# Graph attention on one core: three chunks instead of one gathered in the stage ahead of each layer

## The chip, the cores and the metric

The kernel runs on one core of one Trainium2 chip, in one launch. The metric is the device time of an execution in microseconds. PE is the matrix engine (PEld its weight loads), DVE the vector engine, ACT the scalar engine, POOL GpSimd, SP the sync engine. A q behind a name (POOLq, SPq, ACTq) is that engine's instruction queue. Stages are named by the kernel's functions.

## What is computed

x is 6250 x 256. It is normalised, goes through two graph attention convolutions (4 heads of 64, 100,000 edges sorted by destination, a self loop for every node) and, beside them, a linear attention; the sum is added to x, and a mixture of 16 experts with a last normalisation follows. The change lies in the edges of the two convolutions:

```python
h = (x @ W).reshape(-1, H, C)
e = leaky_relu(alpha_s[src] + alpha_d[dst], NEG_SLOPE)
ex = exp(e - segment_max(e, dst)[dst])
alpha = ex / (segment_sum(ex, dst)[dst] + 1e-16)
out = segment_sum(h[src] * alpha[:, :, None], dst).reshape(-1, H * C) + b
```

## The kernel before

The program is a row of stages, each a block in which the five engines run programs of their own and wait for each other by semaphores. At the end of a stage all engines meet at a barrier; only then does the next begin. The order is prepare, project_inputs, then for each of the two layers **bounds**, **maxima** and **gat_edges**, and last order, experts and finish. maxima does nothing here but read a flag.

Edges are worked off in NC = 98 chunks of CE = 1024 (8 columns of 128). For a chunk SP loads 1024 source indices (idx, line 905) and the destination codes (line 909). POOL then issues 8 indirect DMAs (gather_rows, line 949); each fetches 128 rows of 260 floats, h and alpha_s, from the table of the layer into gathered. There are SLOTS = 3 slots of idx and gathered: chunk c uses slot c % 3, so chunk c can be gathered once chunk c - 3 has been scaled, which the semaphore scaled counts (it starts at 3). DVE makes the selection matrices (lines 1001 and 1019), adds the logits (lines 1013 to 1015, t_e), ACT takes their exponentials (lines 1144 and 1145), DVE scales the gathered rows by them (line 1026), PE sums them per destination (line 1275), and DVE adds the sums to acc (line 1034). Between chunks, per tile of 128 nodes, stand the steps that finish a tile (ACT stores it in the table of the next layer, or in xf_d and moe_d), the linear attention in layer 0 and the gate in layer 1. PE runs spare products (line 1249) while it waits.

The steps of an engine are laid out by skewed: stages with offsets, the first and last turns written out, the middle as a loop over 6 chunks. The number of passes over all chunks is read at run time; with these inputs it is one. At the end of a pass POOL and SP do what the next pass needs (next_dests, next_load), also when there is no next one.

The first chunk of a layer is treated apart. In bounds, where DVE computes bounds of the logits, SP loads idx for chunk 0 (line 577) and POOL gathers it (line 583). In gat_edges gather and load therefore skip chunk 0, and the end of a pass loads and gathers slot 0 again: next_dests waits for the scaling of all chunks, then issues 8 gathers, then waits for the last store (semaphore stored) and computes the next destinations (lines 964 and 945). The last thing POOL does in the stage is to wait until these gathers have landed.

At the start of gat_edges DVE multiplies acc by the nodes' own weights (line 990, four instructions) before its first chunk. In layer 1 ACT issues three loads of expert weights w1, four experts each (line 1197), before its first exponentials:

```python
act.wait_ge(s["codes_in1"], 16)
act.wait_ge(s["idx_in2"], 16)
for e in range(0, NX - 4, 4):
    act.dma_start(w1[:, e:e + 4, :, :], a["L0_ffn_w1"][e:e + 4].rearrange("e (k p) f -> p e k f", p=P)).then_inc(weights_in, 16)
```

Of the kernel before, what the change touches and what calls it, by code (L numbers as in the profile page):

```python
# [33 lines left out]
KT = 8  # L34
CE = KT * P
SLOTS = 3
NC = -(-E // CE)
# [19 lines left out]
def hold(eng, sem, value, tick):  # L57

    eng.wait_ge(sem, value)
    eng.sem_inc(tick, 1)  # L60
# [75 lines left out]
def build(nc, a, out):  # L136
# [6 lines left out]
    srcp = scratch("srcp", (NC * CE,), I32)  # L143
# [6 lines left out]
    weights_in = nc.alloc_semaphore(name="weights_in")  # L150
    firsts = [(nc.alloc_semaphore(name=f"ahead{l}_idx_in0"), nc.alloc_semaphore(name=f"ahead{l}_g_half0"), nc.alloc_semaphore(name=f"ahead{l}_g_in0")) for l in range(2)]

    with ExitStack() as top:
# [20 lines left out]
        landed = sb("landed", [1, 2, XT], I32)  # L174
# [58 lines left out]
        stage(finish, a, moe_d, out, eps, ident, acc)  # L233
    nc.clear_and_free_semaphores([weights_in, *firsts[0], *firsts[1]])

# [317 lines left out]
def bounds(nc, layer, ident, ones, acc, dtab, own, peak, parts, wide, srcp, table, idx, G, ahead, sem):  # L553
# [5 lines left out]
    with ExitStack() as ctx:  # L559
# [15 lines left out]
        @block.sync  # L575
        def _(sp):
            sp.dma_start(idx[:, 0, :], srcp[0:CE].rearrange("(p t) -> p t", t=KT)).then_inc(ahead[0], 16)

        @block.gpsimd
        def _(pool):  # L580
            pool.wait_ge(ahead[0], 16)
            for k in range(KT):
                pool.indirect_dma_start(out=G[:, 0, k, :], out_offset=None, in_=table,
                                        in_offset=bass.IndirectOffsetOnAxis(ap=idx[:, 0, k:k + 1], axis=0)).then_inc(ahead[1 + 2 * k // KT], 16)

# [185 lines left out]
def gat_edges(nc, layer, srcp, table, idx, G, ahead, codes_d, partition, iota, acc, own, peak, parts, windows, attention, last, sem):  # L771
# [6 lines left out]
    with ExitStack() as ctx:  # L778
# [34 lines left out]
        else:  # L813
# [8 lines left out]
            def part(n):  # L822
# [17 lines left out]
            one = sb("one", [P, NT])  # L840
        names = ["idx_in1", "idx_in2", "g_half1", "g_half2", "g_in1", "g_in2", "codes_in0", "codes_in1", "hotT", "hotf", "targets", "dwin", "own", "own_weights",
                 "own_terms", "target_read", "logits", "weights", "scaled", "added", "acc", "pass", "dests", "dest_steps", "vsteps", "logit_steps", "tick",
# [7 lines left out]
        s = {n: sem(f"g{layer}_{n}") for n in names}  # L850
        s["idx_in0"], s["g_half0"], s["g_in0"] = ahead
        FIRST = len(range(0, NC, SLOTS))
        block = ctx.enter_context(nc.Block())
        assert NC == 2 * NT
        PER_STORE = 16 if attention else 32

        def chunks(eng, begin, end, *stages):


            rounds = eng.value_load(passes[0:1, 0:1], min_val=1, max_val=NT + 1)  # L860
            with eng.Fori(0, rounds) as r:
                def told(step):
                    return lambda c, k, u: step(r * NC + c, c, k % SLOTS, k % 2, r * len(range(k % SLOTS, NC, SLOTS)) + u * 2 + k // SLOTS)

                def tile_of(step):

                    def even(c, k, u):
                        if k % 2 == 0:
                            b = k // 2
                            step(r * NT + (u * SLOTS + b), u * SLOTS + b, b, r * len(range(b, NT, SLOTS)) + u)  # L870
                    return even
                begin(r)
                skewed(eng, NC, 2 * SLOTS, 2, 2, [(o, tile_of(step) if by_tile else told(step)) for o, step, *by_tile in stages])
                end(r)
            return rounds
# [20 lines left out]
        def _(sp):  # L896
            def next_load(r):
                hold(sp, s["logits"], r * NC + NC + SLOTS, s["tick"])
                sp.dma_start(idx[:, 0, :], srcp[0:CE].rearrange("(p t) -> p t", t=KT)).then_inc(s["idx_in0"], 16)

            def load(g, c, q, par, use):
                if isinstance(c, int) and c == 0:
                    return
                hold(sp, s["logits"], g + 1, s["tick"])
                sp.dma_start(idx[:, q, :], srcp[ds(c * CE, CE)].rearrange("(p t) -> p t", t=KT)).then_inc(s[f"idx_in{q}"], 16)
# [35 lines left out]
        def _(pool):  # L941
# [10 lines left out]
            def gather(g, c, q, par, use):  # L952
                if isinstance(c, int) and c == 0:
                    return
                pool.wait_ge(s[f"idx_in{q}"], 16 * use + 16)
                hold(pool, s["scaled"], g + 1, s["tick"])
                gather_rows(q)

            def next_dests(r):
                hold(pool, s["idx_in0"], r * (16 * FIRST) + 16 * FIRST + 16, s["tick"])  # L960
                hold(pool, s["scaled"], r * NC + NC + SLOTS, s["tick"])
                gather_rows(0)
                hold(pool, s["stored"], r * (PER_STORE * NT) + PER_STORE * (NT + 1), s["tick"])
                pool.tensor_scalar(behind[:], behind[:], -SPREAD, None, ALU.add).then_inc(s["dest_steps"], 1)
                hold(pool, s["dest_steps"], r + 2, s["tick"])
                dests()
# [3 lines left out]
            dests()  # L970
            rounds = chunks(pool, nothing, next_dests, (0, gather))
            for landed in (s["g_half0"], s["g_in0"]):
                hold(pool, landed, rounds * (8 * KT * FIRST) + 8 * KT, s["tick"])

# [850 lines left out]
```

## Time and profile before

| | |
|---|---|
| median of 3 executions | 2938.16 us (2934.69 to 2940.9) |
| the profiled execution | 2947.23 us, its span 2945.6 us |
| busy, share of the span | PE 78%, PEld 62%, DVE 62%, ACT 31%, POOL 67% |
| mean clock granted to PE | 0.951 |
| gathers | 16 in bounds (line 583), 1568 in gat_edges (line 949) |
| stages, from the timeline | layer 0: bounds from 164.6, gat_edges from 181.9; layer 1: bounds from 1264.0, gat_edges from 1280.8 |

The page gives busy shares over the whole span; they are means over stages with different limits. The busiest engine by these is PE, but a good part of its work are spare products. What bounds a stage is read from who waits for whom in it, and at its borders from the timeline.

### The profile page before, as it was taken

To read this page: it belongs to the slowest core of one execution; us is meant where nothing else is said; L and a number is where in the kernel's file an instruction comes from. 1 tells how busy PE (TensorE), PEld (TensorE's weight loads), DVE (VectorE), ACT (ScalarE), POOL (GpSimd) and SP (SyncE) were. 2 spreads that over 40 slices of the span, in tenths; PEclk is the share of its full clock that TensorE was granted. 3 is DMA by queue.
4 is the path that set the end of the run, shared out by engine and by line. 5 is a ranking of instruction groups with operands and counts; after the bars stand their busy time and mean duration, and the time that the engine had idled before them with its cause. 6 is when DMAs were issued, how large, how long until landed. Compare 5 with 4: busy or idle time off the path is not lost. (4 is left out here: it accounts for less than half of the span.)

```text
span 2945.6 us, 56016 instructions
## 1 busy us (share of the span) xinstructions
PE 2306.1 (78%) x12223; PEld 1818.2 (62%) x12224; DVE 1827.1 (62%) x4382; ACT 925.0 (31%) x2254; POOL 1959.0 (67%) x1934
## 2 busy tenths in 40 slices
PE   1737887878788787728888888888888749999996
PEld 0525555555555555526666666766676539999984
DVE  5655666666666666556666666666666574555545
ACT  0512333333333333301222222222222224444445
POOL 0357777777777777557777777777777406666654
PEclk9969999999999999969999999999999879999998
DMA  3734555555555555345555555555555355565555
GB/s 69 228 102 134 140 139 138 137 138 142 141 139 141 137 137 141 88 152 154 156 150 155 149 153 149 160 148 154 150 155 150 95 149 98 103 107 102 102 90 182
DMA packets 274989, 401.59 MB, mean 136 GB/s; under 512 B 91136, under 2 KB 187799, under 8 KB 274905
## 3 DMA queue, kind: packets, MB, share of 16 engines
q0 software_dynamic: 102496, 253.89, 34.7%
q1 hardware_dynamic: 128745, 101.18, 13.2%
q10 hardware_dynamic: 43680, 45.76, 4.8%
q8 instruction: 25, 0.41, 0.1%
q14 instruction: 43, 0.35, 0.0%
HBM read 346.42 MB, written 54.62 MB: 136 GB/s over the span
## 5 line engine op out<-in xcount | busy, mean ns | idle before, releaser
L949 POOL DMA_INDIRECT gathered<-table,idx x1568 | 1591.8, 1015 | 506.6 <-issue 438.2
L1275 PE MATMUL psA_e<-scaled,hotf 128*128 128x260 f32 x3136 | 748.1, 392 | 67.6 <-issue 62.9
L1275 PEld LDWEIGHTS psA_e<-scaled,hotf 128*128 128x128 f32 x3136 | 588.9, 193 | 159.2 <-issue 74.1
L1249 PE MATMUL psA_e<-mixM,ident 128*128 128x256 f32 x1372 | 348.0, 391 | 91.4 <-DVE hotf L1019 85.2
L1249 PEld LDWEIGHTS psA_e<-mixM,ident 128*128 128x128 f32 x1372 | 254.0, 193 | 153.9 <-issue 122.9
L1144 ACT ACTIVATE scaled<-t_e 128x32 f32<-128x32 f32 x196 | 45.0, 230 | 807.6 <-DVE t_e L1015 801.6
L1688 POOL DMA_INDIRECT moe_d<-xscaled,xtarget x113 | 179.4, 1587 | 122.9 <-DVE xtarget L1632 52.0
L1019 DVE TENSOR_TENSOR hotf<-iota,code_r 128x1024 f32<-128x1024 bf16 x196 | 240.7, 1228 | 0.0
L1026 DVE TENSOR_TENSOR scaled<-gathered,psDW_e 128x2048 f32<-128x2048 f32 x98 | 223.8, 2283 | 25.5 <-ACT psDW_e L1145 25.5
L1026 DVE TENSOR_TENSOR scaled<-gathered,psW_e 128x2048 f32<-128x2048 f32 x98 | 223.7, 2283 | 22.0 <-ACT psW_e L1145 21.5
L1013 DVE TENSOR_TENSOR z_e<-both_e,gathered 128x32 f32<-128x32 f32 x196 | 38.2, 195 | 312.7 <-DMA gathered<-table,idx 302.6
L1660 PEld LDWEIGHTS xpsH<-xxT,w1e 128*128 128x128 f32 x1808 | 220.6, 193 | 6.2 <-ACT xxT L1589 0.4
L1669 PE MATMUL xpsO<-w,hidT 128*128 x904 | 216.0, 382 | 7.4 <-DVE hidT L1621 7.2
L1660 PE MATMUL xpsH<-xxT,w1e 128*128 128x128 f32 x1808 | 221.3, 276 | 0.0
L1034 DVE SCALAR_TENSOR_TENSOR acc<-psA_e,lower,acc 128x260 f32 x196 | 95.8, 489 | 149.7 <-issue 149.4
L1621 DVE TENSOR_SCALAR hidT<-xpsH,b1T 128x128 f32<-128x128 f32 x452 | 127.5, 344 | 91.5 <-issue 46.0
L1144 ACT ACT_TABLE_LOAD x95 | 121.9, 1283 | 195.5 <-DVE t_e L1015 166.5
L1669 PEld LDWEIGHTS xpsO<-w,hidT 128*128 128x128 f32 x904 | 162.8, 190 | 29.2 <-issue 11.1
L1249 PE MATMUL psA_e<-wext,ident 128*128 128x256 f32 x588 | 165.0, 391 | 3.4 <-DVE hotf L1019 3.4
L1283 PE MATMUL psKV<-w 128*128 128x512 f32 x196 | 104.3, 658 | 70.3 <-DVE t_e L1015 70.1
L1289 PE MATMUL psKV<-w 128*128 128x512 f32 x196 | 103.4, 652 | 66.2 <-DVE t_e L1015 66.2
L1249 PEld LDWEIGHTS psA_e<-wext,ident 128*128 128x128 f32 x588 | 112.8, 199 | 64.3 <-issue 55.0
(319 smaller groups left out, 3186.4 us busy)
## 6 DMA issues: line engine op xcount, KB each, us to landing
w<-codes_d SPq DMA_DIRECT2D x196, 256.0 KB, 3.7
gathered<-table,idx POOLq DMA_INDIRECT x1584, 3.3
w<-in_L_ffn_w ACTq DMA_DIRECT2D x8, 2048.0 KB, 19.6
xb<-in_L_ffn_b SPq DMA_DIRECT2D x113, 128.0 KB
table<-acc POOLq DMA_DIRECT2D x49, 130.0 KB
table<-acc ACTq DMA_DIRECT2D x49, 130.0 KB, 2.3
xnT_d<-xnT ACTq DMA_DIRECT2D x49, 128.0 KB, 1.8
w<-xnT_d SPq DMA_DIRECT2D x49, 128.0 KB, 3.7
```

What stands on the lines that cost most here:

```text
L949: pool.indirect_dma_start(out=G[:, q, k, :], out_offset=None, in_=table, in_offset=bass.IndirectOffsetOnAxis(ap=idx[:, q, k:k + 1], axis=0 ...
L1019: dve.tensor_tensor(hotf[:, q, :, :], iota[:].rearrange("p (k f) -> p k f", k=1).to_broadcast([P, KT, P]), code_r[:, ds(c * KT, KT)].rearr ...
L1026: dve.tensor_tensor(scaled[:, par, :, 0:C].rearrange("p k (h c) -> p k h c", h=H), f, w, ALU.mult).then_inc(s["scaled"], 1)
L1144: act.activation(scaled[:, par, :, C:GW], t[:], ACT.Exp).then_inc(s["weights"], 1)
L1249: pe.matmul(psA[:, q, 0:C], ident[:], idle_rhs, start=True, stop=True)
L1275: ins = pe.matmul(psA[:, q, 0:GW], hotf[:, q, k, :], scaled[:, par, k, :], start=(k == 0), stop=(k == KT - 1))
L1283: ins = pe.matmul(psKV[:, 1, :], xnT[b][:, kc * P:(kc + 1) * P], wkvT[:, kc, 1, :], start=(kc == 0), stop=(kc == 1))
L1289: ins = pe.matmul(psKV[:, 0, :], xnT[b][:, kc * P:(kc + 1) * P], wkvT[:, kc, 0, :], start=(kc == 0), stop=(kc == 1))
L1621: dve.tensor_scalar(hidT[:, q % 2, k * P:(k + 1) * P], psH[:, q % 2, k * P:(k + 1) * P], b1T[:, ds(e, 1), k:k + 1].rearrange("p o k -> p ( ...
L1660: ins = pe.matmul(psH[:, q % 2, k * P:(k + 1) * P], w1e[:, q % 2, kc, k * P:(k + 1) * P], xT[:, q % 2, kc, :], start=(kc == 0), stop=(kc = ...
L1669: ins = pe.matmul(psO[:, q % 2, 0:C], hidT[:, q % 2, k * P:(k + 1) * P], w2[:, ds(e, 1), k, :].rearrange("p o f -> p (o f)"), start=(k == ...
L1688: pool.indirect_dma_start(out=moe_d, out_offset=bass.IndirectOffsetOnAxis(ap=target[:, q % 2:q % 2 + 1], axis=0), in_=scaled[:, q % 2, :], ...
```

## The change

The three slots are treated alike. bounds loads and gathers chunks 0, 1 and 2. In gat_edges load and gather skip chunks 0 to 2. The end of a pass loads and gathers three chunks in place of one, in the order of the slots 2, 0, 1 (numbers 98, 99, 100 modulo 3), each as soon as its own slot is free. The semaphores for idx and for the landed gathers of all three slots now live across the stages, one set for each layer. POOL's last wait covers all three slots.

```diff
-    firsts = [(nc.alloc_semaphore(name=f"ahead{l}_idx_in0"), nc.alloc_semaphore(name=f"ahead{l}_g_half0"), nc.alloc_semaphore(name=f"ahead{l}_g_in0")) for l in range(2)]
+    firsts = [{f"{n}{q}": nc.alloc_semaphore(name=f"ahead{l}_{n}{q}") for q in range(SLOTS) for n in ("idx_in", "g_half", "g_in")} for l in range(2)]
 
     with ExitStack() as top:
         def sb(name, shape, dt=F32, ctx=top):
...
         @block.sync
         def _(sp):
-            sp.dma_start(idx[:, 0, :], srcp[0:CE].rearrange("(p t) -> p t", t=KT)).then_inc(ahead[0], 16)
+            for q in range(SLOTS):
+                sp.dma_start(idx[:, q, :], srcp[q * CE:(q + 1) * CE].rearrange("(p t) -> p t", t=KT)).then_inc(ahead[f"idx_in{q}"], 16)
 
         @block.gpsimd
         def _(pool):
-            pool.wait_ge(ahead[0], 16)
-            for k in range(KT):
-                pool.indirect_dma_start(out=G[:, 0, k, :], out_offset=None, in_=table,
-                                        in_offset=bass.IndirectOffsetOnAxis(ap=idx[:, 0, k:k + 1], axis=0)).then_inc(ahead[1 + 2 * k // KT], 16)
+            for q in range(SLOTS):
+                pool.wait_ge(ahead[f"idx_in{q}"], 16)
+                for k in range(KT):
+                    pool.indirect_dma_start(out=G[:, q, k, :], out_offset=None, in_=table,
+                                            in_offset=bass.IndirectOffsetOnAxis(ap=idx[:, q, k:k + 1], axis=0)).then_inc(ahead[f"g_half{q}" if 2 * k < KT else f"g_in{q}"], 16)
...
-        s["idx_in0"], s["g_half0"], s["g_in0"] = ahead
-        FIRST = len(range(0, NC, SLOTS))
+        s.update(ahead)
...
+        def uses_of(q):
+
+            return len(range(q, NC, SLOTS))
+
+        def chunks(eng, begin, end, *stages, head=2):
 
 
             rounds = eng.value_load(passes[0:1, 0:1], min_val=1, max_val=NT + 1)
...
             def next_load(r):
-                hold(sp, s["logits"], r * NC + NC + SLOTS, s["tick"])
-                sp.dma_start(idx[:, 0, :], srcp[0:CE].rearrange("(p t) -> p t", t=KT)).then_inc(s["idx_in0"], 16)
+                for c in range(NC, NC + SLOTS):
+                    q = c % SLOTS
+                    hold(sp, s["logits"], r * NC + c + 1, s["tick"])
+                    sp.dma_start(idx[:, q, :], srcp[q * CE:(q + 1) * CE].rearrange("(p t) -> p t", t=KT)).then_inc(s[f"idx_in{q}"], 16)
 
             def load(g, c, q, par, use):
-                if isinstance(c, int) and c == 0:
+                if isinstance(c, int) and c < SLOTS:
                     return
...
             def gather(g, c, q, par, use):
-                if isinstance(c, int) and c == 0:
+                if isinstance(c, int) and c < SLOTS:
                     return
                 pool.wait_ge(s[f"idx_in{q}"], 16 * use + 16)
                 hold(pool, s["scaled"], g + 1, s["tick"])
                 gather_rows(q)
 
             def next_dests(r):
-                hold(pool, s["idx_in0"], r * (16 * FIRST) + 16 * FIRST + 16, s["tick"])
-                hold(pool, s["scaled"], r * NC + NC + SLOTS, s["tick"])
-                gather_rows(0)
+                for c in range(NC, NC + SLOTS):
+                    q = c % SLOTS
+                    hold(pool, s[f"idx_in{q}"], r * (16 * uses_of(q)) + 16 * uses_of(q) + 16, s["tick"])
+                    hold(pool, s["scaled"], r * NC + c + 1, s["tick"])
+                    gather_rows(q)
...
-            rounds = chunks(pool, nothing, next_dests, (0, gather))
-            for landed in (s["g_half0"], s["g_in0"]):
-                hold(pool, landed, rounds * (8 * KT * FIRST) + 8 * KT, s["tick"])
+            rounds = chunks(pool, nothing, next_dests, (0, gather), head=SLOTS)
+            for q in range(SLOTS):
+                for landed in (s[f"g_half{q}"], s[f"g_in{q}"]):
+                    hold(pool, landed, rounds * (8 * KT * uses_of(q)) + 8 * KT, s["tick"])
```

POOL's instructions at the stage of the bounds of layer 0 (line 583, now 585, is the gather; line 559 the end of the block, 165 the barrier, 680 or 682 the start of maxima). Before:

```order
L467 DMA table<-acc 128x260
L435 UNCONDITIONAL_BRANCH
L165 ISA
L579 UNCONDITIONAL_BRANCH
L583 DMA gathered<-table,idx 128x260 x8
L559 UNCONDITIONAL_BRANCH
L165 ISA
L680 UNCONDITIONAL_BRANCH
```

The change:

```order
L467 DMA table<-acc 128x260
L435 UNCONDITIONAL_BRANCH
L165 ISA
L580 UNCONDITIONAL_BRANCH
L585 DMA gathered<-table,idx 128x260 x24
L559 UNCONDITIONAL_BRANCH
L165 ISA
L682 UNCONDITIONAL_BRANCH
```

The gathers ahead of the barrier are 24 in place of 8.

POOL's instructions at the end of the pass of layer 0 (line 949, now 956, is the gather, 8 for a chunk; line 59 belongs to the waits; 964 and 945, now 973 and 952, are next_dests after the wait for the stores). Before, from the gathers of chunk 96 on:

```order
L59 REGISTER_ALU
L949 DMA gathered<-table,idx 128x260 x8
L59 REGISTER_ALU
L949 DMA gathered<-table,idx 128x260 x8
L59 ISA
L59 REGISTER_ALU
L949 DMA gathered<-table,idx 128x260 x8
L59 ISA
L964 TENSOR_SCALAR behind<-behind 1x1
L59 REGISTER_ALU
L945 TENSOR_SCALAR dest<-iota,behind 1x49
L861 REGISTER_ALU
```

The change, from behind the gathers of chunk 97 on:

```order
L59 ISA
L59 REGISTER_ALU
L956 DMA gathered<-table,idx 128x260 x8
L59 ISA
L59 REGISTER_ALU
L956 DMA gathered<-table,idx 128x260 x8
L59 REGISTER_ALU
L956 DMA gathered<-table,idx 128x260 x8
L59 ISA
L973 TENSOR_SCALAR behind<-behind 1x1
L59 REGISTER_ALU
L952 TENSOR_SCALAR dest<-iota,behind 1x49
```

Between the last gather of the pass's own chunks and the destinations now stand three times 8 gathers, with a wait on indices and one on scaled ahead of each.

## Rows read from the trace of the kernel before

**Rows 1.** The page's part 5, one group: busy, mean ns, idle before, releaser

```profile
L1013 DVE TENSOR_TENSOR z_e<-both_e,gathered 128x32 f32<-128x32 f32 x196 | 38.2, 195 | 312.7 <-DMA gathered<-table,idx 302.6
```

**Rows 2.** POOL's groups in the windows 215.9:1218.5 and 1316.3:2311.3 (layers 0 and 1)

```profile
L949 POOL DMA_INDIRECT gathered<-table,idx x760 | 771.1, 1015 | 231.7 <-issue 213.1 <-DVE scaled L1026 14.6 <-DMA idx<-srcp 4.0
...
L949 POOL DMA_INDIRECT gathered<-table,idx x760 | 763.5, 1005 | 232.6 <-issue 211.6 <-DVE scaled L1026 15.8 <-DMA idx<-srcp 5.2
```

**Rows 3.** Timeline of bounds, layer 0: start, us, engine, line, operation, idle before

```profile
166.44 1.04 POOL L583 DMA_INDIRECT gathered<-table,idx  x1 [8.66 <-DMA idx<-srcp]
...
175.60 0.96 POOL L583 DMA_INDIRECT gathered<-table,idx  x1 [0.30 <-issue]
...
181.89 0.81 SPq L914 DMA_DIRECT2D w<-in_L_gnn_b  x2
```

**Rows 4.** Line 559, the end of bounds, layer 0: durations in ns, start us

```profile
L559 DVEq DRAIN  x1: 10/10/10, 173.7 to 173.7; - x1
L559 POOLq DRAIN  x1: 9801/9801/9801, 169.0 to 169.0; - x1
```

**Rows 5.** Timeline, layer 1: last gather in bounds, first instruction of gat_edges

```profile
1274.93 0.94 POOL L583 DMA_INDIRECT gathered<-table,idx  x1 [0.31 <-issue]
...
1280.80 0.14 POOL L968 IOTA number_i<- 128x16 int32 x1 [4.92 <-POOLq L166]
```

**Rows 6.** Timeline, start of gat_edges, layer 0

```profile
183.78 13.43 DVE L990 TENSOR_TENSOR acc<-acc 128x3136 f32<-128x3136 f32 x4 [0.43 <-ACT acc L1139]
...
189.42 2.01 POOL L949 DMA_INDIRECT gathered<-table,idx  x1 [6.39 <-DMA idx<-srcp]
...
202.48 0.19 DVE L1015 TENSOR_TENSOR t_e<-z_e,both_e 128x32 f32<-128x32 f32 x1
...
204.42 2.29 DVE L1026 TENSOR_TENSOR scaled<-gathered,psDW_e 128x2048 f32<-128x2048 f32 x1 [0.61 <-ACT psDW_e L1145]
...
215.95 0.95 POOL L949 DMA_INDIRECT gathered<-table,idx  x1 [0.30 <-issue]
```

**Rows 7.** Timeline, start of gat_edges, layer 1

```profile
1285.00 0.86 SPq L909 DMA_DIRECT2D w<-codes_d  x2
...
1299.08 0.36 SPq L905 DMA_DIRECT2D idx<-srcp  x1
...
1301.74 0.19 DVE L1015 TENSOR_TENSOR t_e<-z_e,both_e 128x32 f32<-128x32 f32 x1
...
1302.03 0.33 SPq L905 DMA_DIRECT2D idx<-srcp  x1
...
1302.60 7.79 ACTq L1197 DMA_DIRECT2D w<-in_L_ffn_w  x3
...
1313.21 2.29 DVE L1026 TENSOR_TENSOR scaled<-gathered,psW_e 128x2048 f32<-128x2048 f32 x1 [10.14 <-ACT psW_e L1145]
...
1316.32 0.95 POOL L949 DMA_INDIRECT gathered<-table,idx  x1 [1.15 <-DVE scaled L1026]
```

**Rows 8.** Window 1310:1315: PE, PEld, DVE, ACT, POOL busy, clock, DMA share, GB/s

```profile
1310.00:1315.00 5.00, 0.00 (x0) 0.00 (x0) 1.78 (x1) 1.60 (x3) 3.78 (x5) 0.50 1.04 373
```

**Rows 9.** Landings: loads of codes_d in 1316:1328, in 400:600; idx loads in 400:600

```profile
DMA to landing us min/median/max: 6.6/7.0/7.5
...
DMA to landing us min/median/max: 3.2/3.7/4.1
...
DMA to landing us min/median/max: 2.7/3.3/4.3
```

**Rows 10.** Timeline, end of layer 0

```profile
1217.49 0.95 POOL L949 DMA_INDIRECT gathered<-table,idx  x1 [0.30 <-issue]
...
1252.84 0.23 POOL L964 TENSOR_SCALAR behind<-behind 1x1 f32<-1x1 f32 x1 [17.90 <-DMA table<-acc]
...
1257.80 0.69 DVE L1083 COPY mixM<-psM 128x512 f32<-128x512 f32 x1 [3.81 <-PE psM L1327]
```

**Rows 11.** Timeline, end of layer 1

```profile
2347.09 0.23 POOL L964 TENSOR_SCALAR behind<-behind 1x1 f32<-1x1 f32 x1 [18.40 <-DMA moe_d<-w]
```

More of the change, by code:

```diff
@@ L233, in build @@
         stage(finish, a, moe_d, out, eps, ident, acc)
-    nc.clear_and_free_semaphores([weights_in, *firsts[0], *firsts[1]])
+    nc.clear_and_free_semaphores([weights_in, *firsts[0].values(), *firsts[1].values()])
 def prepare(nc, a, srcp, codes_d, partition, ident, identb, ones, iota, eps, code, lower, upper, first_tile, passes,
@@ L840, in gat_edges @@
             one = sb("one", [P, NT])
-        names = ["idx_in1", "idx_in2", "g_half1", "g_half2", "g_in1", "g_in2", "codes_in0", "codes_in1", "hotT", "hotf", "targets", "dwin", "own", "own_weights",
+        names = ["codes_in0", "codes_in1", "hotT", "hotf", "targets", "dwin", "own", "own_weights",
                  "own_terms", "target_read", "logits", "weights", "scaled", "added", "acc", "pass", "dests", "dest_steps", "vsteps", "logit_steps", "tick",
@@ L855, in gat_edges @@
         PER_STORE = 16 if attention else 32
-        def chunks(eng, begin, end, *stages):
+        def uses_of(q):
+            return len(range(q, NC, SLOTS))
+        def chunks(eng, begin, end, *stages, head=2):
             rounds = eng.value_load(passes[0:1, 0:1], min_val=1, max_val=NT + 1)
@@ L872, in chunks @@
                 begin(r)
-                skewed(eng, NC, 2 * SLOTS, 2, 2, [(o, tile_of(step) if by_tile else told(step)) for o, step, *by_tile in stages])
+                skewed(eng, NC, 2 * SLOTS, head, 2, [(o, tile_of(step) if by_tile else told(step)) for o, step, *by_tile in stages])
                 end(r)
```

## The prediction

> **What bounds the kernel now.** I read the page first, then the waits by group, then the timeline at the borders of the stages. In the page's costliest groups the DVE instruction that first touches a gathered chunk (line 1013) sat idle 302.6 us waiting for the gather to land [rows 1]. So for two thirds of the program (216 to 1218 in layer 0, 1316 to 2311 in layer 1) somebody waits for POOL's gathers. Whether POOL itself waits decides what they cost. In each of the two windows POOL issues 760 gathers, chunks 3 to 97 of one layer. In layer 0 they are busy 771.1 us with 231.7 us of idle time ahead of them, in layer 1 763.5 and 232.6 [rows 2]. That is 0.305 us of idle time a gather, and 0.30 us is what POOL leaves between any two gathers, waits or not, as in the bounds [rows 3]; nothing is left over for a wait on DVE. So from chunk 3 to chunk 97 **POOL's issue is the bound**, some 10.5 us a chunk, and the end of a layer moves with the start of chunk 3's gathers. The question is only when chunk 3 starts, and what the stages around it cost.
>
> **What bounds the stage of the bounds.** It holds 8 gathers, from 166.44 to 176.56, 10.12 us [rows 3]. DVE is through at 173.7, where its own drain takes 10 ns, but POOL's drain at the block's end takes 9.80 us, from 169.0 to 178.8, 2.2 us past the end of the last gather [rows 4]. Only then do the barriers run, and the first instruction of the edge stage comes at 181.89. So the stage already ends on POOL, by about 3 us over DVE. Layer 1 looks the same: last gather ends 1275.87, first instruction of the edge stage 1280.80 [rows 5].
>
> **The sum.**
> 1. *Sixteen more gathers in each stage of the bounds.* There is no cover: DVE has ended, and every engine waits at the barrier for POOL. Two chunks at 10.12 us: **+20.2 us a layer**, for everything behind. The two extra index loads are issued 0.35 us apart behind the first, and a chunk's gathers hide them: 0.
> 2. *Chunks 1 and 2 are no longer gathered in the edge stage, layer 0.* Before, chunk 3's first gather starts at 215.95. Now slot 0 is all it waits for: chunk 0's scaling, which starts at 204.42 and ends at 206.71 [rows 6]. From such an end to POOL's next gather it takes 0.8 us (1315.50 to 1316.32 [rows 7]). So it could start at 207.5 of the old time scale: **-8.4 us**. DVE's way to that point does not change: its first 13.43 us (line 990) are its own, and chunk 0 was gathered long before. The slow gathers beside line 990 (2.01 us instead of 0.95 [rows 6]) go away, and that is within the 8.4. Layer 0: +11.8.
> 3. *The same in layer 1.* There chunk 3 starts at 1316.32 and really waited for the scaling of chunk 0, which ended only at 1315.50, because ACT was late by 10.14 us [rows 7]. ACT was busy issuing three loads of the expert weights, 7.79 us from 1302.60 on. It issues them once index load 2 has landed, and that load left at 1299.08. After the change this semaphore is full before the stage starts, so ACT waits only for the codes of chunk 1, issued by 1285.86 [rows 7], landing 3.7 us later [rows 9]: weights from 1289.6 to 1297.4, 4.5 us before t_e is ready at 1301.93. Then the scaling of chunk 0 ends 4.04 us after t_e as in layer 0 (202.67 to 206.71 [rows 6]), at 1305.97, and POOL could start at 1306.8.
>  The price: these weights, 3 x 2.1 MB (four experts of 256 x 512 floats each), fill the DMA engines. At the 373 GB/s of a full window (share 1.04 [rows 8]) they last 16.9 us, to 1306.5. The index load of chunk 3 leaves within that, at 1302.03 [rows 7]. Loads of codes took 7.0 us beside the weights instead of 3.7 [rows 9]; an index load of 3.3 us scaled alike takes 6.2. POOL then starts at 1302.0 + 6.2 + 0.8 = 1309.0: **-7.3 us**. Bounds: 1306.8 if the load is not slowed (-9.5), 1310.3 with the longest landing, 7.5 us (-6.0). I take 1309.0, as the traffic is the same weights. Layer 1: +12.9.
>  On that index load the Trainium skill (DMA: Bandwidth & Descriptors, Queues, rings and completion order) says that each DMA engine goes round its queues packet by packet, so a small load has its turn after one packet of the weights. By that rule alone it would land after little more than 3.3 us, and the sum would be 2.2 us lower. The codes rows, on the same queue, show that the turn costs about 3 us here.
> 4. *Three gathers at the end of a pass in place of one.* Chunk 97's last gather ends at 1218.44. The extra ones now start at once, as chunk 95's slot is free, and take 3 x 10.1 = 30.4 us, to about 1249, 1250.5 at the mean pace of the layer; slot 1 is free (scaling of 97) well before its turn. POOL is next needed when the stores have landed, 1252.84, and the stage ends on DVE's copy at 1257.80 [rows 10]. They are **hidden: 0**, with 2 to 4 us to spare before the store's wait, and 8 before DVE. Without that cover it would be up to 20 us a layer. In layer 1 chunk 97's last gather ends at 2311.3 at the latest (where the window of [rows 2] closes), 30.4 us more is 2341.7, ahead of the 2347.09 at which POOL is next needed [rows 11], with DVE's whole choice of experts still to come: 0.
> 5. *Waits added:* POOL's last holds now look at six landing counts instead of two. The last landing comes 3.3 us after the last gather; 0. Nothing queues behind the added waits on SP (its last loads of the stage).
>
> Sum: 11.8 + 12.9 = **+24.7 us**. The profiled execution took 2947.23 us (span 2945.6), 9.1 above the median of the three runs, so its changed twin should read about 2971.9 (span 2970.3), and the median 2938.16 + 24.7 = **2962.9**.
>
> **The rivals.**
> - *Layer 1 gives nothing back.* ACT's weights do not come earlier, or they delay codes and indices so far that the scaling of chunk 0 still ends near 1315.5. For it: chunk 0 to 2 now compete with weights in full flight. Against: codes of chunks 1 and 2 leave before or as the flood begins. Then layer 1 loses all 20.2: 2938.2 + 11.8 + 20.2 = 2970.2. Chance 0.14.
> - *Faster: the gathers in the bounds are hidden.* If POOL's gathers only had to be queued and not executed before the barrier, the sixteen would run beside barrier, head and line 990, and chunk 3 would start 8.4 and 7.3 us earlier: 2922.5. It decides from about 15 us hidden per layer on. Against it stands the 9801 ns drain, which is exactly the sort of wait that would be missing. The Trainium skill (DMA: Bandwidth & Descriptors, Rules for kernel authors) advises to issue a DMA early and wait late, so that its fixed cost overlaps; by that rule this is the outcome. The trace speaks against applying it, as what is moved is issue time on the engine that bounds the stage, not landing time. Chance 0.04.
> - *About the same:* half of the sixteen hidden, or the early weights help more than I count. Chance 0.03.
> - *The tail shows.* Three gathers plus the drain run past 1257.8, because the table stores and the gathers slow each other. It needs 8 us of slowing in layer 0. Price then 2 to 5 us: 2966. Chance 0.05.
> - My forecast: 0.74.
>
> **Range.** A change within 0.2%, 5.9 us, can't be told from none here. The bounds of layer 1's term give 22.5 to 26.0, the runs scatter by 3 us, and the upper rivals reach 2970. I take 2955 to 2971, which leaves out the faster cases and the top of the first rival. Faster 0.04, same 0.03, slower 0.93.
>
> **What would show it.** In the timeline of the changed kernel: 24 gathers in the bounds, POOL's drain there near 30 us, the edge stage 20.2 us later after the last work of the stage before it. Chunk 3's first gather some 25 us after the edge stage's first instruction in layer 0 and 28 in layer 1 (34.1 and 35.5 now). ACT's three weight loads issued before t_e. POOL without waits until chunk 97, and behind it 24 gathers without a gap. The forecast is wrong if DVE, not POOL, ends the bounds, if the layer between chunk 3 and 97 changes its length by more than 2 us, or if the pass's end grows.

## The result: 0.8% slower, and the profile after

The changed kernel ran in 2966.5 us (median of 4 runs, 2957.7 to 2968.5) beside 2938.5 for the kernel before on the same chip: ratio 1.0083, 95% interval 1.0066 to 1.0100, which is 24.4 us of 2938.2 with an interval of 19.4 to 29.4. The two medians themselves lie 28.0 us apart. Forecast was +24.7. A second job on another chip gave 2960.4 beside 2935.5 (24.9 us), ratio 1.008 [1.0057, 1.0102]. The profiled execution took 2968.5 us with a span of 2966.9, where the forecast said 2971.9 and 2970.3.

**The bounds, layer 0.** The timeline of POOL in the changed kernel (start, us, engine, line, operation, idle before):

```profile
166.88 1.04 POOL L585 DMA_INDIRECT gathered<-table,idx  x1 [8.61 <-DMA idx<-srcp]
...
196.04 0.95 POOL L585 DMA_INDIRECT gathered<-table,idx  x1 [0.30 <-issue]
202.97 0.18 POOL L978 TENSOR_SCALAR behind<-passes 1x1 f32<-1x1 int32 x1 [5.98 <-POOLq L166]
203.25 0.86 POOL L952 TENSOR_SCALAR dest<-iota,behind 1x49 int32<-1x49 bf16 x1
228.65 1.02 POOL L956 DMA_INDIRECT gathered<-table,idx  x1 [24.54 <-DVE scaled L1036]
```

The last gather ends at 196.99, where it ended at 176.56 [rows 3]: 20.4 us later, 0.4 of which was there at the first one. The edge stage's first instruction follows at 202.97 instead of 181.89. Nothing covered the sixteen. The block's end, line 559 (durations in ns of both layers, start in us):

```profile
L559 DVEq DRAIN  x2: 10/10/10, 174.0 to 1282.6; - x2
L559 POOLq DRAIN  x2: 17811/17874/17938, 181.9 to 1290.4; - x2
```

DVE is through at 174.0 and POOL at about 199.8, 2.9 us after its last gather (2.2 before [rows 4]). The distance between the two engines' ends grew from some 5 us to 26.

**The head of the edge stage, layer 0.** DVE's timeline in the changed kernel:

```profile
204.86 13.43 DVE L1000 TENSOR_TENSOR acc<-acc 128x3136 f32<-128x3136 f32 x4 [0.43 <-ACT acc L1149]
...
225.50 2.29 DVE L1036 TENSOR_TENSOR scaled<-gathered,psDW_e 128x2048 f32<-128x2048 f32 x1 [0.61 <-ACT psDW_e L1155]
```

The scaling of chunk 0 ends at 227.79 and POOL issues at 228.65, 0.86 us later; POOL's 24.54 us of idle time above are what the two chunks used to fill. DVE's row of line 1000 is as long as before [rows 6].

**The head, layer 1:**

```profile
1273.47 1.28 SPq L578 DMA_DIRECT2D idx<-srcp  x3
...
1310.92 0.14 POOL L977 IOTA number_i<- 128x16 int32 x1 [5.57 <-POOLq L166]
...
1319.31 5.23 ACTq L1207 DMA_DIRECT2D w<-in_L_ffn_w  x3
1331.87 0.19 DVE L1025 TENSOR_TENSOR t_e<-z_e,both_e 128x32 f32<-128x32 f32 x1
...
1332.16 0.33 SPq L912 DMA_DIRECT2D idx<-srcp  x1
1333.80 2.29 DVE L1036 TENSOR_TENSOR scaled<-gathered,psW_e 128x2048 f32<-128x2048 f32 x1 [0.61 <-ACT psW_e L1155]
...
1338.83 1.15 POOL L956 DMA_INDIRECT gathered<-table,idx  x1 [26.53 <-DMA idx<-srcp]
```

ACT issues the weights well ahead of t_e. DVE's wait for ACT ahead of the scaling fell from 10.14 us [rows 7] to 0.61, and what POOL waits for last is the index load, which took 6.67 us from its issue.

**Chunks 3 to 97.** POOL's groups in the windows of layer 0 and layer 1 (min/median/max ns of one, starts):

```profile
L956 POOL DMA_INDIRECT gathered<-table,idx x760: 942/947/1999, 228.7 to 1227.1; - x190
  issue: 213.3, 700
...
L956 POOL DMA_INDIRECT gathered<-table,idx x760: 942/947/1977, 1338.8 to 2330.3; - x190
```

Ahead of 700 of layer 0's gathers lies nothing but POOL's own gap of 0.30 us. The maximum of 1999 ns beside a median of 947 is taken up with e7 to e11.

**Where the time went**, from the two profiled executions (us after the span's start):

| | before | after | step |
|---|---|---|---|
| layer 0, first gather of chunk 3 | 215.95 | 228.65 | +12.70 |
| layer 0, end of chunk 97's gathers | 1218.44 | 1228.07 | -3.07 |
| index load of layer 1's bounds | 1264.02 | 1273.47 | -0.18 |
| layer 1, first gather of chunk 3 | 1316.32 | 1338.83 | +13.06 |
| layer 1, end of chunk 97's gathers | 2311.24 | 2331.21 | -2.54 |
| first instruction of the order stage | 2364.41 | 2384.27 | -0.11 |
| end of the span | 2945.6 | 2966.9 | +1.44 |

The two heads give +25.8. The stretches from chunk 3 to chunk 97 are 5.6 us shorter although the change doesn't touch them; the experiments below say why these lengths vary. The borders (the index load and the order stage) kept their lengths within 0.2 us. So the two profiled executions differ by 21.3 us, and what the change itself moved is the heads.

### The profile page after: what moved, and what is told of

Its sections match the earlier page's. It is cut to its first block and busy times, and to the rows that moved or that the text cites. A ratio compares the mean times of both kernels' runs of the same rounds, so it can differ in the third digit from the quotient of the medians.

```text
span 2966.9 us, 56070 instructions
## 1 busy us (share of the span) xinstructions
PE 2300.5 (78%) x12223; PEld 1814.3 (61%) x12224; DVE 1824.9 (62%) x4382; ACT 924.3 (31%) x2254; POOL 1972.7 (66%) x1966
## 5 line engine op out<-in xcount | busy, mean ns | idle before, releaser
L956 POOL DMA_INDIRECT gathered<-table,idx x1568 | 1575.8, 1005 | 529.0 <-issue 436.4
L1679 PEld LDWEIGHTS xpsO<-w,hidT 128*128 128x128 f32 x904 | 163.7, 191 | 31.9 <-issue 13.7
L1299 PE MATMUL psKV<-w 128*128 128x512 f32 x196 | 101.0, 639 | 66.0 <-DVE t_e L1025 66.0
L1293 PE MATMUL psKV<-w 128*128 128x512 f32 x196 | 98.7, 627 | 66.1 <-DVE t_e L1025 66.1
```

What stands on the lines that cost most here:

```text
L956: pool.indirect_dma_start(out=G[:, q, k, :], out_offset=None, in_=table, in_offset=bass.IndirectOffsetOnAxis(ap=idx[:, q, k:k + 1], axis=0 ...
L1293: ins = pe.matmul(psKV[:, 1, :], xnT[b][:, kc * P:(kc + 1) * P], wkvT[:, kc, 1, :], start=(kc == 0), stop=(kc == 1))
L1299: ins = pe.matmul(psKV[:, 0, :], xnT[b][:, kc * P:(kc + 1) * P], wkvT[:, kc, 0, :], start=(kc == 0), stop=(kc == 1))
L1679: ins = pe.matmul(psO[:, q % 2, 0:C], hidT[:, q % 2, k * P:(k + 1) * P], w2[:, ds(e, 1), k, :].rearrange("p o f -> p (o f)"), start=(k == ...
```

## The experiments

The medians of e0 to e3 belong to one chip, those of e4 to e7 to a second, e8 to e11 to a third; ratios are to the kernel before in the same job.

**e0_again: the changed kernel, once more, as the mark for e1 to e3.** No edit.

> The changed kernel once more, beside the next three. The forecast's sum says +24.7 us over the kernel before (2963), the first measurement 2966.5. Both theories expect 2960 to 2968; the spread of its runs says what a difference to the next kernels is worth.

Measured: 2960.4 (6 runs, 2950.1 to 2964.6), 1.0080 [1.0057, 1.0102]. In its profile (span 2951.1) chunk 3 starts at 227.94 and 1333.75, but layer 0's stretch takes 994.9 us and layer 1's 983.0, against 999.4 and 992.4. These 13.9 us are most of the 15.8 between two profiled executions of one kernel.

**e1_no_tail: nothing fetched for a next pass.** Index loads and gathers at a pass's end are left out (there is one pass).

```diff
-                for c in range(NC, NC + SLOTS):
-                    q = c % SLOTS
-                    hold(pool, s[f"idx_in{q}"], ...)
-                    hold(pool, s["scaled"], r * NC + c + 1, s["tick"])
-                    gather_rows(q)
```

> The changed kernel without any load or gather for a next pass (48 gathers fewer; the computation here, one pass, is whole). My theory: the 24 gathers at the end of a layer lie under the last stores and DVE's last work, so within 2 us of the changed kernel (about 2964). Rival, the tail pays: the sixteen more gathers at each layer's end are what costs, then this kernel falls back by 10 to 20 us, toward 2940 to 2950. In the timeline my theory wants the stage of the bounds of layer 1 to begin as long after chunk 97's last gather as in the changed kernel (45.4 us), the rival much earlier.

Measured: 2954.0, 1.0061 [1.0042, 1.0079], 6.4 us under e0; the intervals overlap. From the end of chunk 97's gathers to the next stage's first load it took 43.9 us in layer 0 (1225.90 to 1269.77), against 45.4 with the tail and 45.6 before. The border itself is where it differs:

```profile
1266.58 0.69 DVE L1085 COPY mixM<-psM 128x512 f32<-128x512 f32 x1 [3.81 <-PE psM L1329]
1269.77 1.28 SPq L578 DMA_DIRECT2D idx<-srcp  x3
```

That is the timeline of e1: 2.5 us from the end of DVE's last copy to the next stage. In the changed kernel it is 6.3 (1267.19 to 1273.47), in the kernel before 5.5. What holds the border is POOL's drain at the end of the block (line 778 in the kernel before, 780 in the other two; durations in ns of both layers, start in us). Before, changed, e1:

```profile
L778 POOLq DRAIN  x2: 9395/9396/9397, 1253.6 to 2347.9; - x2
```

```profile
L780 POOLq DRAIN  x2: 9214/9218/9221, 1263.3 to 2368.1; - x2
```

```profile
L780 POOLq DRAIN  x2: 7254/7258/7261, 1261.6 to 2363.0; - x2
```

In layer 0 it starts within 1.3 us of the moment at which POOL's wait for the stores ends (1252.84, 1262.08 and 1260.34) and ends at 1263.0, 1272.5 and 1268.8, after DVE's own drain (1258.5, 1267.2, 1267.3); the next stage's first load follows 0.9 to 1.0 us later. So layer 0 ends on POOL, not on DVE's copy, in all three kernels. Gathers at the pass's end lengthen that drain by 2 us, 24 no more than 8; why it takes 7.3 us even without any stays open. In layer 1 DVE's drain ends last (2363.4, 2383.3, 2378.3) and POOL's lies under it. The rival with the tail at 10 to 20 us is out.

**e2_four: eight more gathers in the bounds**, chunk 0's rows once more into slot 2, overwritten by chunk 2's.

```diff
+            pool.wait_ge(ahead["idx_in0"], 16)
+            for k in range(KT):
+                pool.indirect_dma_start(out=G[:, 2, k, :], ... idx[:, 0, k:k + 1] ...).then_inc(s["again"], 16)
...
+                if q == 2:
+                    pool.wait_ge(s["again"], 16 * KT)
```

> The changed kernel with eight more gathers (chunk 0's rows into slot 2, overwritten later) ahead of the others in each stage of the bounds. My theory: every gather ahead of the barrier costs its issue time in full, 10.1 us a layer, so 20.2 us over the changed kernel, about 2984 to 2986, and nothing else in the timeline changes. Rival, part of the issue is covered or the barrier's price is fixed: clearly less, under 10 us.

Measured: 2984.8, 1.0158 [1.0136, 1.0179], 24.4 us above e0 where 20.2 was expected. Its edge stage starts at 213.49 in layer 0, 10.5 after the changed kernel's. Eight more gathers cost their full length twice, and a few us more in the median, which is the order of the scatter. No part of these gathers was hidden in this stage.

**e3_weights_late: ACT issues the expert weights after chunk 3's index load.**

```diff
-                act.wait_ge(s["idx_in2"], 16)
+                act.wait_ge(s["idx_in0"], 32)
```

> The changed kernel, but in layer 1 ACT issues the expert weights only when the index load of chunk 3 has landed (some 28 us after the stage's start) and not at once. My theory: this undoes the gain of layer 1, as ACT is again issuing weights when t_e is ready. Load landed at about 26 us after the stage's first instruction, 7.8 us of issue, 4 us to the end of chunk 0's scaling: chunk 3's first gather some 39 us after the stage's first instruction instead of 28, so 10 us over the changed kernel, about 2974. Rival, the order of the weights does not matter since POOL bounds: no change, 2964 to 2966.

Measured: 2962.4, 1.0088 [1.0069, 1.0107], 2 us above e0 where more was expected. Its head of layer 1:

```profile
1309.18 0.14 POOL L977 IOTA number_i<- 128x16 int32 x1 [5.59 <-POOLq L166]
...
1330.40 0.33 SPq L912 DMA_DIRECT2D idx<-srcp  x1
1332.13 4.89 ACTq L1207 DMA_DIRECT2D w<-in_L_ffn_w  x3
1339.84 2.29 DVE L1036 TENSOR_TENSOR scaled<-gathered,psW_e 128x2048 f32<-128x2048 f32 x1 [8.40 <-ACT psW_e L1155]
1342.62 0.33 SPq L916 DMA_DIRECT2D w<-codes_d  x1
1342.97 1.00 POOL L956 DMA_INDIRECT gathered<-table,idx  x1 [32.41 <-DVE scaled L1036]
```

The mechanism is there: the scaling is late again by 8.40 us behind ACT, and chunk 3 starts 33.8 us after the stage's first instruction, not 27.9. That is 5.9 and not 10 or more, because the index load now landed in 1.7 us (ACT, which waits for it, goes on at 1332.13), and ACT needed only 4.89 us for its issue. The median can't tell 5.9 from the scatter. So beside the weights' traffic that one small load took 5 us longer, issue to waiter, and by this profile issuing them early is still the better order.

**e4_one and e5_two: all three index loads in the bounds, but one or two chunks gathered there, and as many at the end of a pass.** Together with e0 and e2 this is one curve over the number of chunks ahead of the barrier; the kernel before has 2935.5 on one of the two chips and 2935.4 on the other.

```diff
-            for q in range(SLOTS):
+            for q in range(1):
                 pool.wait_ge(ahead[f"idx_in{q}"], 16)
...
-                if isinstance(c, int) and c < SLOTS:
+                if isinstance(c, int) and c < 1:
```

> The changed kernel with all three index loads in the bounds, but only chunk 0 gathered there (and one chunk, slot 0, at the end of a pass); chunks 1 and 2 are gathered at the head of the edge stage, without waiting for an index load. Against the kernel before, POOL starts chunk 1 6 to 8 us earlier after the stage's first instruction, but beside line 990, where one gather took 2 to 3.6 us. My theory: some 5 gathers in those 13.4 us, 11 after it at 1.3 us, so chunk 3 starts 3 to 5 us earlier in each layer: 8 us faster than before, about 2930. If the slow gathers cost nothing in the end it is 14 us, 2924. Rival, the index loads were not what POOL waited for: no change, 2938.

> As the one with one chunk, but chunks 0 and 1 gathered in the bounds. My theory: +10.1 us a layer ahead of the barrier, and chunk 3 starts as early as in the changed kernel (8.4 and 7.3 us earlier against the stage than before): about 4.5 us over the kernel before, 2943, and 20 us under the changed kernel. Rival, the gain grows with each chunk gathered ahead: halfway between before and changed, about 2952.

Measured: e4 2930.8, 0.9984 [0.9971, 0.9997]; e5 2944.2, 1.0028 [1.0016, 1.0040]. The curve: one 2930.8, two 2944.2, three 2960.4, four 2984.8. e4 and e5 came out as expected (2930 and 2943). The index loads alone are worth something, 4.6 us by the medians, with an interval that only just leaves out 0: with one chunk in the bounds POOL starts its second at 184.05 and not 189.42 [rows 6], and chunk 3 starts 2.5 and 3.1 us earlier after the first gather of the bounds. The loss is in the gathers put ahead of the barrier: the ratios of e0 and e4 differ by 0.96%, 28 us for two chunks in two layers.

**e6_before_no_wait: the kernel before, its ACT not waiting for index load 2.**

```diff
-                act.wait_ge(s["idx_in2"], 16)
```

> The kernel before, where ACT in layer 1 no longer waits for index load 2 ahead of its weight loads. My theory: ACT is no longer 10 us late for chunk 0, but POOL, with chunks 1 and 2 still to gather, is busy until 1315.2 anyway; so at most 1.1 us faster, not to be told from before (2938). Rival, the late ACT is itself worth the 8 to 10 us: 2929.

Measured: 2937.5, 0.9998 [0.9986, 1.0009]. ACT's loads went at 1277.53 and the scaling at 1292.35, early, yet chunk 3 started 38.1 us after the stage's first instruction (35.5 before), since POOL had chunks 1 and 2 to gather first. The 2.6 us more are a wait for the index load of chunk 2, which left at 1287.77, beside the weights, and took 8.7 us until POOL went on:

```profile
1296.46 0.94 POOL L949 DMA_INDIRECT gathered<-table,idx  x1 [2.65 <-DMA idx<-srcp]
```

So chunk 3 was held by two things at once, ACT's lateness and POOL's own sixteen gathers, and taking away ACT's alone gives nothing. The change takes away both in the edge stage, and step 3's 7.3 us are what remains of that.

**e7_spread_one: e4 with line 990's four multiplications spread over chunks 0 to 3.** It starts from e4's timeline of POOL, where the first gathers stand still beside them:

```profile
184.05 1.02 POOL L956 DMA_INDIRECT gathered<-table,idx  x1 [0.76 <-issue]
185.38 2.97 POOL L956 DMA_INDIRECT gathered<-table,idx  x1 [0.31 <-issue]
188.66 3.01 POOL L956 DMA_INDIRECT gathered<-table,idx  x1 [0.30 <-issue]
191.98 3.03 POOL L956 DMA_INDIRECT gathered<-table,idx  x1 [0.30 <-issue]
195.31 3.03 POOL L956 DMA_INDIRECT gathered<-table,idx  x1 [0.30 <-issue]
198.64 0.95 POOL L956 DMA_INDIRECT gathered<-table,idx  x1 [0.30 <-issue]
```

```diff
-            for h in range(H):
-                f = acc[:, 0:NT, h * CH:(h + 1) * CH]
-                dve.tensor_tensor(f, f, ..., ALU.mult).then_inc(s["own_terms"], 1)
+            def own_part(g, c, q, par, use):
+                if isinstance(c, int) and c < H:
+                    f = acc[:, 0:NT, c * CH:(c + 1) * CH]
+                    dve.tensor_tensor(f, f, ..., ALU.mult).then_inc(s["own_terms"], 1)
...
```

> As the one with one chunk, and DVE's four multiplications of acc (line 990, 13.4 us ahead of its first chunk) stand one each with the first four chunks, before the first sum is added to acc. (It computes the same as long as there is one pass, as here.) My theory: chunk 0 is scaled 10 us earlier, POOL gathers chunks 1 to 3 without a wait, and chunk 3 starts about 21 to 28 us after the stage's first instruction instead of 34 to 35: 6 to 12 us a layer, 12 to 24 us faster than before, 2914 to 2926. Rival, DVE's later work grows by as much as it saves at the head and DVE becomes the bound in the first chunks: no faster than the one with one chunk.

Measured: 2935.9, 1.0005 [0.9994, 1.0017]: a miss, 5.1 us above e4, whose interval it just touches. Its timeline:

```profile
208.93 3.42 DVE L1003 TENSOR_TENSOR acc<-acc 128x3136 f32<-128x3136 f32 x1
209.60 3.57 POOL L956 DMA_INDIRECT gathered<-table,idx  x1 [0.30 <-issue]
213.47 0.95 POOL L956 DMA_INDIRECT gathered<-table,idx  x1 [0.30 <-issue]
...
219.88 3.42 DVE L1003 TENSOR_TENSOR acc<-acc 128x3136 f32<-128x3136 f32 x1
220.56 3.56 POOL L956 DMA_INDIRECT gathered<-table,idx  x1 [0.31 <-issue]
```

The stall follows the multiplication wherever it is put, and each of these gathers ends 0.82 us after the multiplication beside which it started (213.17 after 212.35, 224.12 after 223.30). So it isn't the place that matters but the pair of instructions, and e8 to e11 test that.

**e8_one_own_in_psum: e4, with the factor of the multiplications read from PSUM.** ACT writes its exponentials there a second time.

```diff
+            act.activation(psO, own[:, 0:NT, :], ACT.Exp).then_inc(s["own_weights"], 1)
...
-                dve.tensor_tensor(f, f, acc[:, 0:NT, C + h:C + h + 1]..., ALU.mult)
+                dve.tensor_tensor(f, f, psO[:, :, h:h + 1]..., ALU.mult)
```

> The kernel that gathers one chunk in the bounds and loads all indices there (2930.8), and ACT writes the nodes' own weights a second time, into PSUM, from where line 990's four multiplications now read them. So these have one operand in SBUF in place of two. My theory on the slow gathers: a gather stands still as long as a DVE instruction with two SBUF operands runs. Then the gathers beside the multiplications take 0.95 us again, 8 us of stalls a layer go, and chunk 3 starts when chunk 0 is scaled: 6 us earlier in layer 0, 5 in layer 1, 2920. Rival, it is the mere length of DVE's instructions or the contention for acc: gathers of 3.0 us stay, 2931.

Measured: 2930.9 beside 2947.2 for the kernel before on this chip, 0.9940 [0.9920, 0.9959]; e4's ratio was 0.9984, so 0.44% more, some 13 us; on the scale of the expectation (2938) it is 2920.6, as expected. Its timeline:

```profile
184.86 13.41 DVE L1002 TENSOR_TENSOR acc<-acc,psF 128x3136 f32<-128x3136 f32 x4 [0.66 <-ACT psF L1152]
185.98 0.97 POOL L957 DMA_INDIRECT gathered<-table,idx  x1 [0.31 <-issue]
187.25 0.95 POOL L957 DMA_INDIRECT gathered<-table,idx  x1 [0.30 <-issue]
188.51 0.95 POOL L957 DMA_INDIRECT gathered<-table,idx  x1 [0.30 <-issue]
```

DVE takes as long as before, 13.41 us, and the gathers take 0.95. From the stage's first gather to chunk 3's it now takes 23.9 us in layer 0 and 27.2 in layer 1; in e4 it was 29.7 and 30.3. So the profile shows 8.9 of the 13 us.

**e9_before_iota_in_psum: the kernel before, and DVE's comparison (hotf, line 1019) reads its row of numbers from PSUM.**

```diff
+            dve.tensor_copy(psI, iota[:]....to_broadcast([P, SLOTS, P])).then_inc(s["lifted"], 1)
...
-                dve.wait_ge(s["added"], g + 1)
-                dve.tensor_tensor(hotf[:, q, :, :], iota[:]..., code_r..., ALU.is_equal)
+                dve.wait_ge(s["added"], g + 2)
+                dve.tensor_tensor(hotf[:, q, :, :], psI[:, (q + 1) % SLOTS, :]..., code_r..., ALU.is_equal)
```

> The kernel before; DVE's comparison of line 1019 (hotf from iota and code_r, 1.23 us, once a chunk) reads iota as floats from PSUM in place of SBUF, and waits for one chunk's sum more. My theory: this is the instruction that meets a gather in nearly every chunk and makes it 1.7 us long; from chunk 3 to 97 gathers lose 48.7 us in layer 0 and 41.1 in layer 1 against 0.95 us each. Without it most of that goes: 55 to 75 us faster, 2865 to 2880, and 10.1 us a chunk. Rival, the slow gathers come from the scaling (2.28 us, one SBUF operand) or from elsewhere: no change, 2936.

Measured: 2857.0 beside 2947.2, 0.9703 [0.9683, 0.9722], 87 us of 2938 and more than expected. First the timeline of the kernel before at one chunk, then e9's at another:

```profile
1210.15 1.22 DVE L1019 TENSOR_TENSOR hotf<-iota,code_r 128x1024 f32<-128x1024 bf16 x1
...
1210.48 1.70 POOL L949 DMA_INDIRECT gathered<-table,idx  x1 [0.30 <-issue]
```

```profile
409.27 1.23 DVE L1022 TENSOR_TENSOR hotf<-psA_e,code_r 128x1024 f32<-128x1024 f32 x1
...
409.64 0.95 POOL L950 DMA_INDIRECT gathered<-table,idx  x1 [0.30 <-issue]
```

In both the gather starts about 0.35 us into the comparison. Counted over the whole trace of the kernel before, 206 gathers start while a comparison runs; 146 of them take more than 1.0 us, up to 2.0, and each of these ends 0.82 us after the comparison's end. Of the 133 that were already running when a comparison started, none takes more than 1.0 us. In e9 190 gathers start while a comparison runs, and the longest takes 0.95. So e9 did not win by moving the comparison out of the gathers' way (it also waits for one sum more); they still meet, and no longer stop each other.

And POOL's groups of e9 in the windows of layer 0 and layer 1:

```profile
L950 POOL DMA_INDIRECT gathered<-table,idx x760: 942/946/1188, 215.6 to 1168.3; - x190
...
L950 POOL DMA_INDIRECT gathered<-table,idx x760: 942/946/1170, 1267.2 to 2218.5; - x190
```

At 0.95 us each, 760 gathers would be busy for 722.0 us. In the kernel before they are busy 49.1 and 41.5 us longer (51 and 34 of them take over 1.3 us); the expectation above has both sums 0.4 lower. In e9 they are busy 722.5 and 721.0 us, so nothing is lost. The stretches shrink from 1002.5 and 994.9 us to 953.7 and 952.2.

**e10_one_both_in_psum: e8 and e9's edit together**, that is one chunk in the bounds, all index loads there, both operands in PSUM.

> Both operand changes on the kernel that gathers one chunk in the bounds and loads all indices there. If the two savings add: 15 from the head and the loads, 55 to 75 from the comparison, 2850 to 2865. Rival, with POOL faster PE or DVE becomes the bound in parts of a layer and the sum is less than that of the two alone.

Measured: 2841.9, 0.9644 [0.9625, 0.9664], 105 us under the kernel before, better than expected and the fastest of all. The two savings add: 0.60% for e8 and 2.97% for e9, 3.56% together. The rival that PE or DVE would become the bound is out.

**e11_three_iota_in_psum: the changed kernel with e9's edit.**

> The changed kernel with the comparison's iota in PSUM. The change's own price does not depend on the slow gathers in my theory: 23 to 27 us over the kernel before with the same edit, so about 2890 to 2905. Rival, the changed kernel's loss comes in part from slower gathers in the layer: then the difference of the two shrinks below 20 us.

Measured: 2887.4, 0.9799 [0.9779, 0.9819], 30.4 us above e9. With no slow gathers, layer 0's stretch from chunk 3 to 97 takes 954.8 us and layer 1's 955.0, against 953.7 and 952.2 in e9, so the change's price stands there nearly without the scatter. Chunk 3 starts 13.7 us later in layer 0 (229.38 to 215.64) and, with that included, 27.4 in layer 1 (1294.57 to 1267.20), of which 1.1 is layer 0's longer stretch: 26.3 us for the two heads, within the 23 to 27 expected. The medians' 30.4 lies above it; 3.9 us of that are the two stretches. The rival, a difference below 20 us, is out.

## Why the prediction was right

Forecast +24.7 us, measured +24.4 by ratio (interval 19.4 to 29.4), 28.0 between the medians, 24.9 in the second job; the time lies in the range and in the case held likeliest. That two of these agree with the forecast to half a microsecond is luck: the runs do not measure so finely, and in the two profiles +25.8 at the heads stands beside -5.6 in stretches that the change does not touch. What bears the forecast out are the heads, +12.7 and +13.1 for +11.8 and +12.9.

1. *Sixteen more gathers without cover:* said 20.2 a layer; 20.0 in the rows of layer 0 and 19.8 in those of layer 1 (30.1 us from 166.88 to 196.99 and 29.9 from 1275.50 to 1305.36, less 10.12 and 10.04 before). Shown by e2, e4 and e5 as well: each chunk moved ahead of the barrier costs 13 us or more of the whole. The rival of hidden gathers is out. The advice of the Trainium skill (DMA: Bandwidth & Descriptors, Rules for kernel authors) to issue early and wait late is about a DMA's fixed setup cost and is not refuted: what was moved early here was 1.25 us of the issuing engine per gather, ahead of a barrier, and where only the index loads were moved (e4) the kernel gained. One sign was told wrongly. POOL's drain reads 17.9 us and not near 30, for it begins at 181.9, not at 169; its end, 2.9 us past the last gather, is what counts. (The prediction's "about 3 us over DVE" before goes by POOL's last gather; by the two drains it was 5.1.)
2. *Layer 0's head:* said -8.4, thus +11.8 in all. Chunk 3 came 12.7 us later. Of the 0.9 too much, 0.4 was there before the bounds; from the last gather to the edge stage's first instruction it took 0.65 longer (5.98 for 5.33), and the gathers took 0.2 less. The 25 us after the stage's first instruction are 25.7.
3. *Layer 1's head:* said -7.3, thus +12.9; measured +13.06, with the weights 8.4 us into the stage (said 8.8), t_e ready at 21.1 (21.1) and chunk 3 at 27.9 (28). The chosen 7.0 us for index load and reaction were 6.67. From the Trainium skill's rule (DMA: Bandwidth & Descriptors, Queues, rings and completion order) that a DMA engine turns from queue to queue packet by packet, the prediction had inferred a landing after little more than 3.3 us. The row stands against that inference, as does e6 with 8.7 us; how the queues took turns these rows do not show. e3 gives the other end, 1.7 us with no weights in flight. The rival "layer 1 gives nothing back" wanted the scaling to stay late; DVE's wait for ACT went from 10.14 to 0.61.
4. *The tail hidden:* 24 gathers ran without a gap to 1259.04 and the wait for the stores was released at 1262.08, so 3.0 us were to spare, within the 2 to 4 said. Said 0; the two profiles give -0.2 and -0.1. But the prediction had the end of layer 0 wrong: it let the stage end on DVE's copy, with 8 us to spare for POOL. The stage ended on POOL's drain, which follows the wait for the stores (9.4 us of it before, 9.2 after, see e1). So POOL had no slack beyond those 3 us, and by these rows a tail longer by more than that would have moved what comes behind it. That e1's median is 6.4 us under e0's is more than its profile shows (1.5 us in layer 0, nothing in layer 1), and how much of it is real stays open.
5. *Waits added:* 0, and nothing in the rows speaks against it.

What the prediction did not see lies between the heads. It named a layer changing its length by more than 2 us as a sign against it. By that sign the forecast would have been called wrong: the lengths changed by 3.1 and 2.5 us. They changed by another 13.9 in e0 with the same code, so the sign was badly chosen, and the length belongs to neither kernel. The gaps ahead of the gathers, without the wait ahead of the first, add up to 231 us in each layer of before, after and e0 and to 231 to 234 in e9; from the changed kernel to e0 the gathers' busy time falls by 4.5 and 9.3 us, which is the 13.9. What varies is how many gathers start beside a comparison of DVE, and how early in it. So "POOL's issue is the bound" was right, and left out that 90 us of it, 4.5% of the two stretches, were gathers standing still, in plain sight as a mean of 1015 ns [rows 2] where a gather in the bounds takes 0.96 us [rows 3].

## What to carry to other kernels

Work that an engine issues one by one costs its full length ahead of a barrier at which that engine is already the last, however early its data are wanted; move what only has to land (the index loads, e4, -4.6 us), and leave the issue where others work beside it. Before pricing a move, look at the maximum beside the median in the group that bounds the kernel: instructions of one shape that sometimes take twice their time may wait for something no semaphore shows, and taking that away (with one chunk in the bounds, e10, -105 us) was worth four times what the move cost. Ask of each border which engine's drain ended last, not which did the last work. Where one kernel's executions differ by ten microseconds, compare the stretch that differs, and price a change by the rest.

## What the runs showed of the hardware

A gather on POOL that starts while DVE runs a long instruction with both operands in SBUF stands still until that instruction ends: it takes 3.0 us, at most 4.1 (e4), instead of 0.95 beside multiplications of 3.42 us each, up to 2.0 beside the 1.22 us comparison, and ends 0.8 to 0.9 us after it. A gather that is already running when the comparison starts is not slowed (133 in the kernel before). With one operand in PSUM the same DVE work takes as long (13.41 us, 1.21 to 1.23 us) and the gather 0.95. The length of a DVE instruction alone is not the cause: beside the scaling, 2.28 us with one operand in PSUM, 292 gathers start in the kernel before and the longest takes 1.01 us, and beside the 1.19 us sum of line 1059, which has a single operand, in SBUF, 48 start and none takes over 0.95. In e9 the row of numbers also became f32 (bf16 before); in e8 the type stayed, so it is not the type either.

The nearest rule is what the Trainium skill (SBUF — State Buffer, SBUF: two separate sides) says of the port pair that DVE and GpSimd share, an exclusive lock taken also by a DVE operation "with two SBUF inputs (only against a GpSimd op that reads SBUF)", which the one that starts first holds for its whole instruction. The rows agree in one direction, with an indirect DMA's issue as the GpSimd operation; whether it counts because it reads its indices from SBUF no run tests. In the other direction they do not: 132 comparisons start in the kernel before while a gather is running, each within 0.2 us of the start of the step ahead of it, and take 1.21 to 1.26 us, so DVE waits for no gather. The prediction had taken the 2.01 us gather of [rows 6] for a matter of the stage's head alone.

An index load of 4 KB took 6.67 us (changed kernel) and 8.7 us (e6) from its issue to POOL's start beside 6 MB of weights, and 1.7 us to ACT's start without them (e3).

POOL's drain ends the bounds 2.2 us after its last gather with one chunk, 2.9 with three and 3.2 with four (e2). At the end of the edge stage it takes 9.2 to 9.4 us though the gathers are long issued, and 7.3 us where the pass's end has none (e1).
